# Relative attention in a four-layer kernel: transposed probabilities in pairs over two PSUM banks, position product at the end of a step

## The reference

```python
x = _layernorm(src, ln1_g, ln1_b)
q, k, v = (x @ w).reshape(Bs, Ss, 16, 8)      # w in wq, wk, wv; 16 heads of 8
pos = jnp.arange(Ss - 1, -Ss, -1)
pe = concat([sin(ang), cos(ang)])             # of the positions
p = (pe @ wp).reshape(2 * Ss - 1, 16, 8)
ac = einsum("bihd,bjhd->bhij", q, k)
bd_full = einsum("bihd,phd->bhip", q, p)
bd = bd_full[:, :, i, i - j + (Ss - 1)]
att = softmax((ac + bd) / sqrt(8))
attn_out = einsum("bhij,bjhd->bihd", att, v).reshape(Bs, Ss, 128) @ wo
src = src + attn_out
```

## Time and profile before

| what | us |
|---|---|
| runs (three) | 4686.77, 4683.23, 4682.64 |
| median | 4683.23 |
| the profiled execution's own time | 4708.06 |
| its span, first to last instruction | 4706.2 |
| TensorE matmul busy in the span | 3839.9 (82%) |
| VectorE busy | 2675.1 (57%) |
| ScalarE busy | 2196.8 (47%) |
| GpSimd busy | 1812.5 (39%) |

### The profile page before, as it was taken

How to read it: one execution, slowest core, us unless ns; L and a number is a source line. 1 busy time by engine, 2 the same in 40 slices (tenths; PEclk the granted TensorE clock), 3 DMA queues, 4 the chain that set the end, 5 groups by cost and what they waited for, 6 DMA issues and landing times. The chain is left out here.

```text
span 4706.2 us, 80320 instructions
## 1 busy us (share of the span) xinstructions
PE 3839.9 (82%) x27592; PEld 2767.0 (59%) x27592; DVE 2675.1 (57%) x6451; ACT 2196.8 (47%) x5289; POOL 1812.5 (39%) x1981
## 2 busy tenths in 40 slices
PE   4899999168399999699999688886799999995482
PEld 2666666025156666466666478875477777774361
DVE  2444444724256665466666466665488888885133
ACT  2455656034256665345444344444566666661120
POOL 2545544403056666233332000000366666662405
PEclk6999999588689999799999899998899999996795
DMA  1545554200300000000000100000122222223121
GB/s 40 139 125 135 137 135 122 85 8 1 72 1 1 1 1 1 10 1 2 1 2 1 37 0 0 0 0 17 40 74 76 77 76 76 74 77 104 44 70 62
DMA packets 233046, 226.84 MB, mean 48 GB/s; under 512 B 59321, under 2 KB 177145, under 8 KB 232314
## 3 DMA queue, kind: packets, MB, share of 16 engines
q1 hardware_dynamic: 226010, 208.68, 16.2%
q0 software_dynamic: 4096, 8.40, 0.6%
q10 hardware_dynamic: 2592, 5.26, 0.3%
HBM read 168.26 MB, written 54.00 MB: 47 GB/s over the span
## 5 line engine op out<-in xcount | busy, mean ns | idle before, releaser
L2126 DVE TENSOR_TENSOR_SCAN a_h<-a_dA,a_dBu_psum 128x512 f32<-128x512 f32 x512 | 595.7, 1204 | 164.3 <-issue 106.7
L1127 POOL TENSOR_SCALAR a_probs<-a_probs,a_row_inv 128x128 f32<-128x128 f32 (+1 forms) x512 | 382.7, 766 | 321.1 <-DVE a_row_inv L1113 321.1
L2083 POOL TENSOR_TENSOR a_h<-a_h,main_g 128x512 f32<-128x512 f32 x256 | 385.1, 1507 | 268.9 <-DVE a_h L2126 258.8
L1625 DVE SCALAR_TENSOR_TENSOR m_acc<-m_o_psum,m_gate,m_acc 128x128 f32<-128x128 f32 x992 | 297.8, 346 | 117.5 <-PE m_o_psum L1589 117.4
L1850 PE MATMUL a_dBu_psum<-a_B_diag,a_dt_u_turned 64*128 64x128 f32 x4096 | 316.9, 289 | 20.9 <-DVE a_h L2126 20.1
L1589 PEld LDWEIGHTS m_o_psum<-m_values,m_hidden 128*128 128x128 f32 x2048 | 313.4, 197 | 29.8 <-ACT m_hidden L1607 2.3
L1581 PE MATMUL m_h_psum<-m_x,m_keys 128*128 128x256 f32 x1024 | 327.9, 411 | 0.0
L1607 ACT ACTIVATE m_hidden<-m_h_psum 128x256 f32<-128x256 f32 x512 | 196.7, 384 | 264.8 <-PE m_h_psum L1581 264.7
L1589 PE MATMUL m_o_psum<-m_values,m_hidden 128*128 128x128 f32 x2048 | 313.8, 279 | 0.0
L1452 POOL TENSOR_TENSOR r_position_q<-r_turned_q 128x512 f32<-128x512 f32 x128 | 160.1, 1272 | 388.7 <-DVE r_turned_q L1497 388.7
L1850 PEld LDWEIGHTS a_dBu_psum<-a_B_diag,a_dt_u_turned 64*128 64x128 f32 x4096 | 257.9, 188 | 75.1 <-issue 70.1
(11 more groups left out here) (549 smaller groups left out, 9050.5 us busy)
## 6 DMA issues: line engine op xcount, KB each, us to landing
main_g<-a_b_c_rows SPq DMA_DIRECT2D x256, 256.0 KB, 3.1
a_band_rows<-main_g SPq DMA_DIRECT2D x64, 512.0 KB, 2.6
a_B<-a_band_rows SPq DMA_DIRECT2D x192, 128.0 KB, 3.0
a_A<-a_band_rows SPq DMA_DIRECT2D x192, 128.0 KB, 3.0
f_x_rows<-f_zero ACTq DMA_DIRECT2D x16, 320.0 KB, 8.0
f_x_expert<-f_x_rows SPq DMA_DIRECT2D x16, 320.0 KB
f_y_rows<-f_y_expert SPq DMA_DIRECT2D x16, 320.0 KB, 2.2
f0b_stage_w<-L_ffn_up_weights SPq DMA_DIRECT2D x9, 512.0 KB
```

The lines of the kernel that those rows point to most:

```text
L1127: ins = nc.gpsimd.tensor_scalar(pr[:, h % NPR, tile[t]], pr[:, h % NPR, tile[t]], rinv[:, p % NST, q:q + 1], None, ALU.mult)
L1625: ins = nc.vector.scalar_tensor_tensor(out=acc[:, t, :], in0=o, scalar=gate[:, t, e:e + 1], in1=acc[:, t, :], op0=ALU.mult, op1=ALU.add)
L2083: tt(h[:, r, :, :], h[:, r, :, :], Cs[:, g % NCS, :, :], ALU.mult).then_inc(hc_pool, 1)
L2126: nc.vector.tensor_tensor_scan(flat, dA[:, M % NDA, q, k, :, :].rearrange("p n t -> p (n t)"), db[:, 2 * (g % 2) + k, :], 0.0, ALU.mult, A ...
```

## The change

Only the order of work and the place of one tile change; no instruction that computes is added or removed.
- Transposed heads 1 and 3 go to bank 1 of `zb` (the second position bank) in place of `tb`; heads 0 and 2 stay in `tb`.
- TensorE's order is `logit(p)`, `add_position(p, 0)`, side product, transposes 0 and 1, `add_position(p, 1)`, transposes 2 and 3, `weigh(p-2)`, `position(p+2)`.
- `transpose(k, 1)` waits for bank 1 of `zb`: for the rotation, in a "qk" step for VectorE's copy of k, in a "v" step for ScalarE's copy of v, and for the copy of head 3 of the step before. `position` waits for the copy of head 3 in place of the copies of k and v.
- ScalarE's order is exponentials 0 and 1, copy of q or v, copy of head 0, exponentials 2, copy of head 2, exponentials 3.

```diff
--- before.py
+++ after.py
@@ -1287,9 +1287,10 @@
                     for what, q in beside(p):
                         if what == "qk":
                             pe.wait_ge(q_sb, q + 1)
-                            pe.wait_ge(k_sb, q + 1)
-                        else:
-                            pe.wait_ge({"v": v_sb, "st": st_sb, "bc": o_ready, "y": y_out}[what], q + 1)
+                        elif what != "v":
+                            pe.wait_ge({"st": st_sb, "bc": o_ready, "y": y_out}[what], q + 1)
+                    if p >= 1:
+                        pe.wait_ge(pt_hi, 2 * p)
                     for half in range(2):
                         for g in range(4):
                             i = g // 2
@@ -1324,11 +1325,26 @@
 
                 def transpose(k, g):
                     pe.wait_ge(probs, 8 * k + 2 * g + 2)
-                    if g or k:
-                        pe.wait_ge((pt_hi, pt_lo)[g % 2], 2 * k + (0, 1, 1, 2)[g])
+                    if g == 0 and k:
+                        pe.wait_ge(pt_lo, 2 * k)
+                    elif g == 1:
+
+                        bank_free(k + 1, 1)
+                        for what, q in beside(k + 1):
+                            if what == "qk":
+                                pe.wait_ge(k_sb, q + 1)
+                            elif what == "v":
+                                pe.wait_ge(v_sb, q + 1)
+                        if k:
+                            pe.wait_ge(pt_hi, 2 * k)
+                    elif g == 2:
+                        pe.wait_ge(pt_lo, 2 * k + 1)
+                    elif g == 3:
+                        pe.wait_ge(pt_hi, 2 * k + 1)
+                    dst = zb[:, 1, :] if g % 2 else tb[:, 0, :]
                     for kt in range(2):
                         for t in range(2):
-                            ins = nc.tensor.transpose(tb[:, 0, kt * T + t * P:kt * T + (t + 1) * P],
+                            ins = nc.tensor.transpose(dst[:, kt * T + t * P:kt * T + (t + 1) * P],
                                                       pr[:, k % 2, g, t, kt * P:(kt + 1) * P], c["ident"][:])
                     ins.then_inc(tr_mm, 1)
 
@@ -1357,24 +1373,21 @@
                 for p in range(LAST + 1):
                     if p < NQ:
                         logit(p)
-                    if 1 <= p <= NQ:
-                        transpose(p - 1, 0)
-                    if p < NQ:
                         add_position(p, 0)
                     for what, b in beside(p):
                         make(what, b, p)
                     if 1 <= p <= NQ:
+                        transpose(p - 1, 0)
                         transpose(p - 1, 1)
                     if p < NQ:
                         add_position(p, 1)
                     if 1 <= p <= NQ:
                         transpose(p - 1, 2)
-                    if p + 2 < NQ:
-                        position(p + 2, p)
-                    if 1 <= p <= NQ:
                         transpose(p - 1, 3)
                     if 2 <= p < NQ + 2:
                         weigh(p - 2)
+                    if p + 2 < NQ:
+                        position(p + 2, p)
 
             @block.scalar
             def _(act):
@@ -1422,17 +1435,18 @@
                 for p in range(LAST + 1):
                     if p % NG == 2 and p // NG >= 1:
                         keep_o(p // NG - 1)
-                    if 1 <= p <= NQ:
-                        turn(p - 1, 0)
                     if p < NQ:
                         exps(p, 0)
                         exps(p, 1)
                     for what, b in beside(p):
                         keep(what, b)
                     if 1 <= p <= NQ:
+                        turn(p - 1, 0)
+                    if p < NQ:
+                        exps(p, 2)
+                    if 1 <= p <= NQ:
                         turn(p - 1, 2)
                     if p < NQ:
-                        exps(p, 2)
                         exps(p, 3)
 
             @block.gpsimd
@@ -1507,7 +1521,7 @@
                     dve.wait_ge(tr_mm, 4 * k + g + 1)
                     if k >= 2:
                         dve.wait_ge(pv_mm, k - 1)
-                    nc.vector.tensor_copy(pt[:, k % 2, g, :, :].rearrange("p k t -> p (k t)"), tb[:, 0, :]).then_inc(pt_hi, 1)
+                    nc.vector.tensor_copy(pt[:, k % 2, g, :, :].rearrange("p k t -> p (k t)"), zb[:, 1, :]).then_inc(pt_hi, 1)
 
                 keep("qk", 0)
                 for k in range(2):
```

## The result

The changed kernel takes 4719.26 us (median of 6, 4714.18 to 4724.26), the kernel before 4682.32 (median of 6 on the same chip): a ratio of 1.0079, 95% interval 1.0066 to 1.0092, so 31 to 43 us slower. The forecast was 4711, 28 us slower, with a range of 4698 to 4732.

The account below looks back on a forecast made before the run. TensorE and ScalarE were taken as level bounds of relative attention. Waits for shared-bank copies add 31.1 us, other steps -1, tail -2: +28 us on 4683.23 gives 4711 us, range 4698 to 4732.

Parts of the forecast that it names:

- What bounds: Relative attention: TensorE's blocks and ScalarE's chain both take 5.16 us from second position addition to next logits; saving on TensorE alone is worthless.
- Changes of tiling: TensorE's transposes, merged in pairs: two of nine tiling changes go per step, 0.17 us each, 0.34 us in all.
- A1 to L: From adding position the second time to the next logits block: ScalarE's chain sets 5.30 us, 0.14 longer than before.
- The wait of L: Logits block on TensorE: waits some 0.3 us for the probabilities in every step.
- "qk" and "v": Key- and value-projection steps: head 1's transposes wait for copies out of the shared bank; steps 0.49 and 1.58 us longer.
- The clock: Rival: new idle in value-projection steps halves TensorE's clock once per sequence of four steps, 27 us more, 4738 us; 10%.
- A clock under 1: Sign of being wrong: granted clock below full within the 658 us window of relative attention.
- The sum: Whole kernel: copies 31.1 us, the two other step kinds -1, tail -2; together +28 us, 4711 us.
- "y" and "st": The two step kinds without key or value copies: a wash, 9.84 to 9.81 and 11.32 to 11.29 us; 32 x -0.03 = -1 us.
- behind the last logits: Tail of relative attention: with two banks the last four transposes no longer take turns, 2 us back.
- hand-over: From the end of a copy to the start of the TensorE block waiting for it: 0.12 us.
- its own mechanism: Waits for key and value copies, with the rest a wash: 4705 to 4718 us, 70%.

Follow-up runs that it names:

- exponentials first: Changed kernel, but ScalarE takes all exponentials of heads 2 and 3 before copying transposed head 2: 4703.81 us, ratio 1.0049 to the kernel before.
- bank 0: Changed kernel, but keys and values are projected into bank 0 and VectorE copies them and the queries: 4669.33 us, ratio 0.9978 to the kernel before.
- both mends: Changed kernel with keys and values in bank 0 copied by VectorE, and exponentials 2 and 3 before head 2's copy: 4682.97 us, ratio 0.9946 to before.
- Second bank only: Kernel before in its own block order; only transposed head 1 goes to the second position bank, with the needed waits: 4751.02 us, ratio 1.0144.
- copy of head 2 first: Changed kernel, but ScalarE copies head 2 before exponentials 2 and 3, as before the change: 4743.57 us, ratio 1.0077; again 4715.52 us, 1.0078.
- filled version: Changed kernel with ScalarE copying head 2 before exponentials 2 and 3, and head 0's transposes repeated three times more in value-projection steps: 4704.01 us, ratio 1.0055.

## Why the prediction was right

*What bounds.* Right. TensorE and ScalarE were level at 5.16 from A1 to L, and each experiment that touched one alone showed the other: merged blocks without the exponentials first gave nothing (bank 0, steps level with before), the shorter chain gave until TensorE's 5.08.

*Changes of tiling.* Right, a little large. T0 adds 0.44 us between A0 and A1 ("y" 2.99 to 3.43) and T2 and T3 stand 0.39 apart, where a block with its own change took 0.59, and L passes to A0 at the same 1.10 us. With both mends they give 0.25 to 0.26 us a step of the 0.34 worked out; the missing 0.09 is the 5.08 against 4.99 from A1 to L. The Trainium skill, "TensorEngine Tiling (Array Packing)", "Tiling Modes", says that a change of mode drains the array. The rows agree in so far as a change costs 0.15 to 0.2 us; they don't show the draining, and in the change as made it decided nothing.

*A1 to L.* Forecast 5.30, measured 5.29. The wait of L was forecast 0.3 and was 0.2, since P came 0.06 later than added up and took 0.03 longer.

*"qk" and "v".* Right in place and mechanism, a little small: A1 came 0.10 and 0.11 us later than forecast. The copy ended where forecast, and T1 started 0.22 us behind it instead of 0.12 (2240.01 to 2240.23). The 0.12 was read where the awaited semaphore is the last one in the queue; behind the wait for the copy stands another, for the odd copy of the step before. It is 3 us in 30 steps. "Second bank only" has no such wait behind the one for the copy, and there T1 starts 0.11 behind the copy's end in both kinds of step (2205.07 to 2205.18), so that its A1 in "qk" comes 4.35 after A0, the forecast's 4.36. P, too, whose wait for the copy of head 3 is its last, starts 0.11 behind that copy in the changed kernel. This fits the second wait as the cause; T1 follows another block in "second bank only", so it is not shown alone.

*The clock.* This is the step that the forecast had wrong. It gave 10% to a fall in each sequence and put a few falls at nothing, because the new idle is shorter than one that the kernel bore. It fell in 2 of 15 "v" steps of the profile, 1.57 us each, 3 us. The falls came at the new 1.5 us wait and not at the longer one of 1.7 us in the "st" steps, so that the shorter idle was not the safer one. A clock under 1 was named as a sign of being wrong, and it was seen. This is the term that was left out of the sum.

*The sum.* 15 x (0.58 + 1.69) = 34.1, "y" and "st" -0.6, clock 3.1, and -2.5 for the rest (-3.1 behind the last logits, where -2 was forecast, and +0.6 in the first steps): 34.1 us measured in the stage. The forecast's 28 lacks 3 for the hand-over and 3 for the clock. The median, 4719.26, lies in the range of 4698 to 4732 and 1 us above the narrower 4705 to 4718 that the forecast had for its own mechanism. Under the profiler 4736 was forecast and 4720.66 measured: the profiled execution of after lay 1.4 us above its median, and not 25 as that of before did. This touches neither the stage nor the medians. The runs' 31 to 43 us holds the stage's 34; whether the few us between 34 and the median's 37 are more falls in other executions or noise stays open, as only one execution of it is profiled.

## What to carry to other kernels

A second bank that is shared is not free: list who still reads it when the new writer comes, and read from the timeline when that reader gets to it. Here the reader had four exponentials ahead of it in its queue, and 1.3 us came back from moving one copy in ScalarE's program.

Where two engines' chains between two points are equal to a few hundredths of a us, shortening one shows nothing, and it can look like a failed idea. Shorten the other one too before dropping it: the merged blocks were worth 0.02 us a step alone and 0.25 with the exponentials first.

A gain in a step can be eaten by the clock. Look at the granted clock of every stretch after a reordering, not at its mean over the span, which was 0.904 both in the changed kernel, where it fell twice in the steps, and in the filled version of "copy of head 2 first", where it never did.

## What was not expected of the hardware

Waits are taken here between matmuls. The granted clock fell at waits of 1.5 us (in 2 of 15 "v" steps of the changed kernel, 2 of 15 with steps 0.24 us shorter, "exponentials first", 7 of 15 with steps 0.14 us shorter, in both profiles of "copy of head 2 first"), and in 13 of 15 at waits of 1.84 us (second bank only). It never fell at the "st" steps' 1.7 us, in the eleven profiles that have this wait. In the "st" steps the wait is followed by transposes alone (the sums, then T1, in the new order T0 and T1); in the "v" steps of the changed kernel it has the projections and T0 before it and T1 behind. So the length of the wait does not decide alone. In "copy of head 2 first" two sequences took 88.8 us, with one fall in them, and it fell at exactly every second sequence, in two profiles. That suggests that a fall depends also on where the wait lies in time; no run here tests it.

Transposes held the clock up: sixteen in place of four took all falls away, seven in one kernel and two in another. The Trainium skill, "TensorE: Matmul & The Clock Gate", Part 4, says that transposes do not count as busy in the same way; no run here supports that for these fp32 transposes, and these two speak against it.

The kernel before took 4681 us on one chip, 4679 on another and 4708 on a third, 0.6% more. A difference of one per cent has to be taken from runs side by side.
